# Dummy matmuls ahead of the first maximum steps and of the normalized transposes of a four-layer gated cross-attention kernel

## The reference, cut to what matters

```
for l in range(4):
    x = x + tanh(g_xattn[l]) * xattn_l(layernorm(x), ctx)
    x = x + tanh(g_ffn[l])   * ffn_l(layernorm(x))

xattn: softmax(Q @ K.T / sqrt(8)) @ V, then an output projection
  layer 0: keys gated by a sigmoid of an energy input
  layer 1: two attentions with shared Q, added: one over the 256 tokens of x itself
           (local), one over the 1601 context keys (global)
  layer 3: a mask over (query, key) from an input
ffn:  layer 0: ternary weights, gelu, layernorm;  layers 1 and 3: top-2 of 8 experts;
      layer 2: a product with a matrix made from a Fourier transform
```

## Time and profile before

| | |
|---|---|
| three runs | 1693.75, 1697.20, 1698.21 us; median 1697.2 |
| the profiled execution | 1704.45 us |
| its span, first to last instruction | 1702.7 us |
| mean granted TensorE clock | 0.913 of full speed |
| busy | PE 89%, DVE 77%, ACT 68%, POOL 9% of the span |

### The profile page before, as it was taken

The page is one execution under the profiler, slowest core; times in us unless marked ns, Lnnn a source line. Parts: engine busy times, 40 slices in busy tenths (PEclk is TensorE's granted clock), DMA queues, the critical chain, the costliest instruction groups (busy, mean ns, idle before and its releaser), DMA issues.

```text
span 1702.7 us, 45795 instructions
## 1 busy us (share of the span) xinstructions
PE 1511.9 (89%) x15521; PEld 655.5 (38%) x15521; DVE 1305.1 (77%) x2224; ACT 1163.9 (68%) x2209; POOL 149.2 (9%) x246
## 2 busy tenths in 40 slices
PE   6689999978689999995997799999788999999967
PEld 4323333346223333334675133333353444444345
DVE  5599999555778999954784899998347888888168
ACT  3259899842356999982994399899354777777636
POOL 6000000012000000002221000000100000000012
PEclk9779999989578999996999699999787999999879
DMA  9921221105301212110115221221161111111001
GB/s 274 281 64 55 65 64 54 62 1 149 115 25 44 62 58 65 55 46 1 50 64 160 83 63 54 65 65 33 40 206 37 53 43 43 54 43 44 14 17 34
DMA packets 85286, 119.39 MB, mean 70 GB/s; under 512 B 18967, under 2 KB 57390, under 8 KB 85198
## 3 DMA queue, kind: packets, MB, share of 16 engines
q1 hardware_dynamic: 81694, 109.05, 21.5%
q0 software_dynamic: 2560, 8.20, 1.5%
q10 hardware_dynamic: 944, 0.93, 0.2%
HBM read 83.48 MB, written 34.49 MB: 69 GB/s over the span
## 4 chain that ended last, share of the span: by engine, by line
PE 64%; DVE 16%; issue 8%; SPq 5%; ACT 3%; DMA 2%; POOL 1%; DVEq 0%; ACTq 0%; POOLq 0%
PE pv_bank L1582 21%; DVE mx L1127 10%; PE exp_ring L1570 10%; PE score_ring L1544 5%; PE exp_ring L1562 4%; PE score_ring L1540 4%; PE score_ring L1810 3%; PE exp_ring L1821 3%; PE exp_ring L1567 3%; DMA k_d<-k2c 2%; PE pv_bank L1658 1%; PE score_ring L1465 1%; PE exp_ring L1472 1%; PE score_ring L1723 1%; PE exp_ring L1647 1%
## 5 line engine op out<-in xcount | busy, mean ns | idle before, releaser
L871 ACT ACTIVATE early<-exp_ring 128x512 f32<-128x512 f32 (+1 forms) x1664 | 884.1, 599 | 230.0 <-PE exp_ring L1570 111.2
L1127 DVE TENSOR_REDUCE mx<-score_ring 128x2 f32<-128x802 f32 (+1 forms) x768 | 703.4, 985 | 33.6 <-PE score_ring L1544 33.5
L1582 PE MATMUL pv_bank<-early,vg 128*32 128x256 f32 x6656 | 528.3, 396 | 0.9 <-issue 0.4
L1544 PE MATMUL score_ring<-kp,qp 64*128 64x401 f16 (+1 forms) x1536 | 311.3, 351 | 35.8 <-DVE mx L1127 32.3
L1570 PE MATMUL exp_ring<-qp,kp 64*128 64x512 f16 (+1 forms) x1248 | 313.6, 390 | 11.2 <-DMA qp<-ms 7.0
L1582 PEld LDWEIGHTS pv_bank<-early,vg 128*32 128x32 f32 x6656 | 139.0, 108 | 239.7 <-issue 117.7
L1570 PEld LDWEIGHTS exp_ring<-qp,kp 64*128 64x128 f16 (+1 forms) x1248 | 95.3, 95 | 188.8 <-ACT early L871 151.1
L1544 PEld LDWEIGHTS score_ring<-kp,qp 64*128 64x128 f16 x1536 | 76.0, 93 | 195.7 <-DVE mx L1127 172.8
L1540 PE MATMUL score_ring<-kp,qp 64*64 64x400 f16 (+1 forms) x1024 | 137.6, 356 | 11.9 <-DVE mx L1120 9.0
L1562 PE MATMUL exp_ring<-qp,kp 64*64 64x512 f16 x832 | 130.0, 400 | 2.8 <-DMA qp<-ms 2.8
L1567 PE MATMUL exp_ring<-ctxT,mask_eye 64*64 64x512 f16 x800 | 126.3, 386 | 0.0
(11 more groups left out here) (271 smaller groups left out, 1505.5 us busy)
## 6 DMA issues: line engine op xcount, KB each, us to landing
kp<-k_d SPq DMA_DIRECT2D x128, 400.2 KB
k_d<-k1c SPq DMA_DIRECT2D x32, 400.2 KB, 6.6
ctxT<-ctxT_d SPq DMA_DIRECT2D x12, 800.5 KB, 6.0
qp<-q_d SPq DMA_DIRECT2D x512, 12.0 KB
k_d<-k2c SPq DMA_DIRECT2D x16, 400.2 KB, 6.7
k_d<-v_loc POOLq DMA_DIRECT2D x12, 400.2 KB, 8.8
ctxT_d<-ctxT SPq DMA_DIRECT2D x4, 800.5 KB, 6.1
o_all<-in_ctx SPq DMA_DIRECT2D x4, 768.0 KB
```

The lines of the kernel that those rows point to most:

```text
L871: act.activation(pt[g][0:rows_, 2 * h:2 * h + 2, :], bank[0:rows_, :].rearrange("p (i q) -> p i q", q=S), ACT.Exp).then_inc(exped, 1)
L1127: dve.tensor_reduce(dst, src, AX.X, ALU.max).then_inc(score_free, 1)
L1544: ins = pe.matmul(pa[slot][:, z, 0:w], qp1[par][rows_, i, qt * P:qt * P + P], kp1[par][rows_, at:at + w], start=True, stop=True)
L1582: ins = pe.matmul(po[R * j:R * j + R, 0:S], vg[par][0:rows_, s, j, :], pt[g][0:rows_, j, :], start=(s == 0), stop=(s == r.kt - 1))
```

## The change

A helper, `warm(bank, times)`, issues matmuls whose result nobody reads: the fp16 identity as weights and the identity four times over as the moving operand, 128 x 128 over 512 columns, into a bank that the next real matmul overwrites. It is called at four kinds of place. In `normT`, for s from 1 on, 14 of them stand ahead of the first wait for xn. In the first fill of the runs of layers 0, 2 and 3, 28 stand ahead of unit 0's first step and two ahead of each of the other 15; in the local run 28 ahead of the first step and four ahead of each other one that stands before the first fill. In all four layers two stand ahead of each of the eight steps of unit 1. In `piece` they come after the wait for the score slot and ahead of the wait for the loaded keys. Nothing else changes.

```diff
+WARM_STEP, WARM_START, WARM_NORM = 2, 28, 14
...
+            def warm(bank, times):
+
+                for _ in range(times):
+                    pe.matmul(bank.rearrange("p (k d) -> p k d", d=P), ident16[:, :],
+                              ident16[:, :].unsqueeze(1).broadcast_to([P, 4, P]), start=True, stop=True)
+
             def normT(s):
+                if s:
+                    warm(PB[2], WARM_NORM)
                 for T in range(NT):
                     pe.wait_ge(ln_xn, NT * s + T + 1)
...
-                def piece(n, par, k, first=False, half=0):
+                def piece(n, par, k, first=False, half=0, extra=0):
...
                     j = k - (k > r.turn)
                     pe.wait_ge(score_free, use + FREE_SCORE - 1)
+                    warm(pa[slot][:, 0, :], extra)
                     if k == 0:
                         pe.wait_ge(in1[par], IN_DMAS * (r.l0 + n - par + 2))
...
+                    if w < BEFORE[LEAD]:
+                        warm(pa[w % 2][:, 0, :], 2 * WARM_STEP if w else WARM_START)
                     if g == 0 and z == 0:
                         pe.wait_ge(lin[b], 32)
...
                     for k, j in r.pieces(first=True):
-                        piece(0, 0, k, first=True)
+                        piece(0, 0, k, first=True, extra=WARM_STEP if j else WARM_START)
...
                 for k in range(r.ahead):
-                    piece(1, 1, k)
+                    piece(1, 1, k, extra=WARM_STEP)
```

## The result

The changed kernel takes 1726.3 us (median of four runs, 1723.2 to 1729.1) against 1695.9 for the kernel before: a ratio of 1.0165, 95% interval 1.0132 to 1.0199. Run once more later beside the kernel before, it took 1719.6 against 1697.3: 1.0130 (1.0104 to 1.0155). It is 22 to 30 us slower, and the forecast of 1696 was wrong; the range ended at 1708. So I compare with both.

A forecast was written before the change was run, and what follows sets the result against it. VectorE was taken to bound the runs' first steps, PE at half clock the loops and local run. Cost 31.0 against gain 32.6 gave -1.6 us, from the median 1695.6, say 1696; range 1685 to 1708.

The forecast's parts named there:

- The 28 ahead of a run: Starts of four attention runs: nothing hides them, 24.2 us, plus 4 for two clock falls, cost 28.2.
- With the clock up, the PE-bound stretches halve: Loops behind the first steps of layers 0, 2 and 3: gains of 3.4, 4.2 and 2.1, together 9.7 us.
- Two or four ahead of a step: Maximum steps: period 0.93 us with two dummies, about 1.27 with four in the local run; cost 2.8 us.
- The masked first steps: Layer 3's first steps, all PE: from 1.38 to 1.2 us each, gain 2.1 us.
- The local run: Layer 1's local units: from 3.97 to 2.6 or 2.7 us each at full clock, gain 12.5 us.
- was cold before only because nothing had raised it: Layer 1's local loop: ground given for the clock staying up without dummies inside it, on which the 12.5 us rest.
- `heads_out`: End of the local run: 32 transposes at 0.124 instead of 0.229 us, 3.4 us on the path; 2.9 taken.
- The norms: 14 dummies ahead of seven normalized transposes: no cost, higher clock for what follows, gain 5.4 us, 8.6 at most.
- The local run didn't fall back: Rival on layer 1: the clock falls within the first local units, the 12.5 us go, 1708; chance 0.20.
- the clock didn't stay up at all starts: Rival: the clock falls at no start and holds through all norms, 1687; chance 0.28.
- the third: Rival: the clock falls during the normalized transposes, the norms give 1 us, time 1700; chance 0.08.
- The fourth: Rival: dummies don't raise the clock within the steps, 1.4 to 1.5 us a step, above 1730; chance 0.07.

The follow-up runs named there:

- e8: e3 with 56 dummies in place of the 28 ahead of each run of layers 0, 2 and 3: 1737.1 us against e3's 1719.5.
- e12: The changed kernel profiled once more, no edit: 1719.6 us against 1697.3 for the kernel before.
- the first pair: Traces compared: the kernel before as first profiled, against the changed kernel's first profiled execution; +18.7 us in sum.
- e6: Changed kernel without the 28s; 15 (layer 1) and 10 (layer 3) hidden in the end of `kv`, fewer dummies elsewhere: 1694.4 us against 1697.8, ratio 0.9983.
- e5: The kernel before profiled once more, no edit: 1699.3 us.
- e1: Changed kernel with only the 14 dummies ahead of each normalized transpose left: 1691.5 us against 1696.5 for the kernel before, ratio 0.9963.
- e4: Changed kernel without the 28 ahead of layers 0, 2 and 3, two a step kept: 1710.0 us against 1696.5 for the kernel before, ratio 1.0051.
- the second pair: Traces compared: e5 against e12, the later executions of the kernel before and the changed kernel; +20.2 us in sum.
- e3: Changed kernel with dummies in layers 0, 2 and 3 only (28, two a step), no 14: 1719.5 us against 1696.5 for the kernel before, ratio 1.0127.
- e10: Kernel before plus the 14 at all seven norms, ten hidden in layer 3, two on layer 1's eight steps: 1689.5 us against 1697.3, ratio 0.9946.
- e9: Changed kernel without the dummies ahead of the steps, 28s and 14s kept: 1714.2 us against 1697.3 for the kernel before, ratio 1.0096.

## Why the prediction was wrong, point by point

**The 28 ahead of a run** (forecast 28.2) measured 30.4 and 27.3, and e8 shows the price of one, 0.216 us, on the path. I had assumed slow first dummies at two of the three starts behind an idle stretch. In the first execution they were slow at all three: 8.81, 7.89 and 7.89 us against 6.20 in layer 0. In e12's they were slow ahead of the local run alone, 9.02; layer 2's, for one, took 6.20:

```profile
941.05 6.20 PE L1444 MATMUL score_ring<-ident 128*128 128x512 f16 x28 [2.20 <-DVE k2c L1058]
```

This largest term was right. How many of the dummies run slow differs from one execution to the next, so that the sum came this close is in part luck. The error is in what the forecast set against it.

**"With the clock up, the PE-bound stretches halve"** (9.7) is the step that failed first. They were PE-bound, but not by much: in the same rows VectorE is busy 6.09 of 7.00, 6.32 of 8.50 and 3.10 of 4.30 us. If PE's part vanished, 0.9 + 2.2 + 1.2 = 4.3 us were the most to be had in these windows. Measured were 1.6, 1.1 and 1.2 us in the first pair and 2.2, 0.5 and 1.2 in the second, 3.9 both times (in layer 0 VectorE waited once more behind the window, at 104). The window 107 to 114 of the changed kernel, VectorE 6.92 of 7.00, shows the next bound at work. In layer 2 the clock also fell once more behind the steps (0.81 from 973 to 982).

**Two or four ahead of a step** (2.8) measured 9.8 in both pairs. I took 0.43 for a pair. In the timeline it stands from 83.51 to 84.04, when the scores behind it start: 0.53. The round of two slots takes 1.97 us, that is 0.98 + 0.53 + 0.34 and 0.12 left for hand-overs, and not twice 0.93; the local one takes 2.70, not twice 1.27. The dummies ahead of the eight steps of layers 0, 2 and 3 stood in no term of the sum; they cost 0.7, 0.7 and 0.6 us.

**The masked first steps** were to fall to 1.2 us and stand at 1.36, PE-bound still: the two dummies take as much as the clock gives back (16.2 us for 12 steps after 16.6). With nothing between the steps, and the clock up from the ten dummies ahead of them, they take 0.96 (e6): once the clock was up, the step needed none.

**The local run** (12.5) gave 13.6 against the execution that the forecast read and 6.6 against another. The mechanism was right, its clock stayed at 1.00 from the first unit without dummies in the loop. That the loop "was cold before only because nothing had raised it" was not: it raises its clock by itself, sooner or later (e5). (Nine units at 1.3 are also 11.7, not the 11.5 of the sum.) The size was read from one execution, and the reference of the forecast, the median of the runs, was another: I subtracted the 7.25 us between them from the result and left the whole gain in.

**`heads_out`** (2.9) was right: 3.2. **The norms** (5.4) measured 3.9 and 4.4 in the pairs and 5.0 alone (e1), whose interval holds all of these. They give it at four of the seven places only, 0.7 to 1.7 us each. The windows of two of the seven, after the earlier trace rows; the first three rows are layer 2's, the last two layer 1's:

```profile
901.70:904.60 2.90, 2.90 (x18) 1.31 (x15) 2.53 (x9) 0.00 (x0) 0.00 (x0) 1.00 0.00 0
904.60:907.20 2.60, 0.32 (x2) 0.00 (x0) 2.51 (x16) 0.00 (x0) 1.87 (x3) 1.00 0.00 0
907.30:914.10 6.80, 5.90 (x12) 2.52 (x12) 3.15 (x10) 1.82 (x3) 1.15 (x1) 0.50 0.00 0
...
396.70:399.60 2.90, 2.90 (x16) 1.36 (x16) 2.55 (x12) 0.00 (x0) 0.60 (x3) 1.00 0.00 0
399.60:403.00 3.40, 2.94 (x13) 1.55 (x12) 1.57 (x7) 1.20 (x2) 0.80 (x1) 1.00 0.00 0
```

In layer 2 the dummies come at the head of the gap, PE then idles 2.3 of 2.6 us, and the transposes and queries run at 0.50 as before: "nothing where the clock falls in the idle rest after the dummies", as the forecast had it. In layer 1 they fill the gap, and the transposes directly behind them keep 1.00. Longer than there, transposes stand alone in the local `heads_out`: 32 of them with a wait between the halves. In the changed kernel, behind the dummies of the eight steps, the clock stayed at 1.00 through them:

```profile
519.30:524.00 4.70, 3.41 (x30) 2.94 (x28) 3.32 (x14) 0.00 (x0) 0.00 (x0) 1.00 0.00 0
```

The Trainium skill ("TensorE: Matmul & The Clock Gate", Part 4: PE-mode transpose) says that full clock doesn't engage for transposes, which don't count as a busy PE in the same way. By that rule the seven norms would give about 1 us; e1 measured 5.0, and the window above doesn't show the clock falling under transposes. The row that the prediction held against the rule is less clear than it said: from 511.7 to 520.2 the transposes ran at 0.50 throughout, and 1.00 is seen only behind their end. Whether transposes alone raise the clock, no run here settles.

**The rivals.** None happened. The local run didn't fall back, the clock didn't stay up at all starts, and the norms gave 3.9 to 5.0 us, not the 1 of the third. The fourth, that dummies don't raise the clock within the steps, is what e4 shows in layer 3 at 2.35 us a step, but only without the 28. The case that came, a start that costs what was said and gains that the next engine swallows, stood in no rival, though its numbers stood in the earlier trace rows.

Taken together, in the second pair: 7.8 us at the loops and masked steps, 7.0 in the steps, 5.9 in the local run, 1.0 at the norms and 1.3 in the small shifts were missed, 0.9 at the starts and 0.3 at `heads_out` went the other way: 21.8, from -1.6 to +20.2.

## What to carry to other kernels

Where a stretch is bound by an engine at a low clock, read the second engine's busy time in the same window before pricing the clock: the gain ends there, and here it ended after some 4 of 9.7 us. Here a dummy paid only where it was issued while the engine waited anyway and ended where the real work began: 28 behind the last wait cost their whole time, ten ahead of it in layer 3 nothing that the trace shows, and 14 at the head of a long gap were lost by its end. And a gain read from one profiled execution belongs to that execution; a second profile of the unchanged kernel is the cheapest experiment there is.

## What the runs showed that I had not expected

The local loop, which holds no dummies in any of these kernels, raises its own clock where it starts at half: after nine units in the first execution, five in others (e1, e3, e6, e10), three in e5 and e9 and one in e8. But layer 3's masked steps with two dummies each, PE busy 28.00 of 28.00 us at 0.50, don't (e4), in five runs of ten by the times. A busy engine alone doesn't tell which way it goes; what does was not tried.
